# Storing the first softmax maxima by key head, with a shorter lead of maxima before the first scores

## The reference, cut to what matters

```python
q = (x @ Wq + bq).reshape(4, 512, 32, 8)
k = (x @ Wk + bk).reshape(4, 512, 8, 8)      # v likewise; 4 query heads share one key head
attn = softmax(q @ k.T / sqrt(8))            # over 512 keys, per batch and head
out = (attn @ v).reshape(4, 512, 256) @ Wo + bo
```

## Time and profile before

| | |
|---|---|
| median of three executions | 3713.92 us (3711.85 to 3724.83) |
| the profiled execution | 3757.11 us, of which the span from the first to the last instruction is 3755.4 us |
| first maximum of the stage to the last exponential | 1244.3 to about 1731 us of the span |
| first attend of batch 0 | 1274.5 us |
| TensorE, VectorE, ScalarE, GpSimd busy over the whole span | 88%, 70%, 52%, 26% |
| granted TensorE clock, mean of the span | 0.933 of full speed |

### The profile page before, as it was taken

How to read it: one execution, slowest core, us unless ns; L and a number is a source line. 1 busy time by engine, 2 the same in 40 slices (tenths; PEclk the granted TensorE clock), 3 DMA queues, 4 the chain that set the end, 5 groups by cost and what they waited for, 6 DMA issues and landing times. The chain is left out here.

```text
span 3755.4 us, 65204 instructions
## 1 busy us (share of the span) xinstructions
PE 3320.6 (88%) x22154; PEld 2203.1 (59%) x22154; DVE 2622.5 (70%) x8703; ACT 1937.4 (52%) x5275; POOL 990.8 (26%) x960
## 2 busy tenths in 40 slices
PE   6999999986997899997899999988798759999975
PEld 4666676664554344444566676665454437888753
DVE  5888888775444777782788888876444567777765
ACT  4667677654222266675576777655222115555531
POOL 3212112233444001012221212143444333222113
PEclk8999999997999689998999999998999769999986
DMA  4140400012755222302060500011656400000010
GB/s 127 58 160 23 148 1 1 23 44 86 190 90 112 69 53 57 71 3 91 1 216 1 169 1 1 4 44 50 203 90 121 100 1 15 1 15 4 1 33 23
DMA packets 202239, 234.78 MB, mean 63 GB/s; under 512 B 20662, under 2 KB 188536, under 8 KB 201080
## 3 DMA queue, kind: packets, MB, share of 16 engines
q1 hardware_dynamic: 170968, 190.48, 16.7%
q0 software_dynamic: 30944, 40.14, 6.3%
HBM read 98.13 MB, written 133.73 MB: 62 GB/s over the span
## 5 line engine op out<-in xcount | busy, mean ns | idle before, releaser
L1773 ACT ACTIVATE p_prob<-bank,p_small 128x256 f32<-128x256 f32 (+3 forms) x1280 | 647.2, 515 | 151.9 <-DVE p_small L1945 146.7
L1945 DVE CUSTOM_DVE_ANT_0 bank<-bank,p_mask 128x256 f32<-128x256 f32 (+3 forms) x1280 | 579.5, 490 | 145.6 <-PE bank L1516 96.0
L2292 POOL TENSOR_TENSOR p_tm<-p_rope_a,p_rope_b 128x512 f32<-128x512 f32 x192 | 246.3, 1283 | 1273.7 <-DVE p_rope_b L1925 1271.0
L1778 ACT ACTIVATE p_prT<-bank 128x512 f32<-128x512 f32 x752 | 427.4, 602 | 249.5 <-PE bank L1525 203.7
L1516 PE MATMUL bank<-p_k,p_q 64*128 64x256 f32 (+3 forms) x3840 | 530.1, 348 | 20.1 <-ACT p_prob L1773 18.3
L1525 PE MATMUL bank<-g_ident,p_prob 128*128 128x128 f32 x3008 | 448.0, 288 | 66.7 <-DVE p_prob L1954 26.2
L1525 PEld LDWEIGHTS bank<-g_ident,p_prob 128*128 128x128 f32 x3008 | 337.7, 144 | 164.4 <-issue 57.9
L1534 PE MATMUL bank<-p_prT,p_v 128*64 128x512 f32 (+1 forms) x1504 | 431.7, 619 | 1.7 <-issue 1.3
L1954 DVE TENSOR_SCALAR p_prob<-p_prob,p_small 128x256 f32<-128x256 f32 (+3 forms) x1280 | 413.1, 386 | 11.3
L1516 PEld LDWEIGHTS bank<-p_k,p_q 64*128 64x128 f32 (+1 forms) x3840 | 340.0, 189 | 124.8 <-issue 70.7
L1991 DVE TENSOR_REDUCE p_nmax<-bank 128x1 f32<-128x512 f32 x512 | 320.5, 683 | 71.9 <-PE bank L1575 69.9
(11 more groups left out here) (288 smaller groups left out, 6220.7 us busy)
## 6 DMA issues: line engine op xcount, KB each, us to landing
sorted<-p_blank SPq DMA_DIRECT2D x32, 2304.0 KB, 19.3
p_w<-in_L_ffn_w SPq DMA_DIRECT2D x96, 256.0 KB, 4.5
p_h_in<-sorted SPq DMA_DIRECT2D x158, 144.0 KB
p_k_st<-k_saved SPq DMA_DIRECT2D x16, 288.0 KB
p_q_st<-q_saved SPq DMA_DIRECT2D x16, 288.0 KB
g_stage<-in_L_ffn_wq SPq DMA_DIRECT2D x8, 512.0 KB
g_stage<-in_L_ffn_wo SPq DMA_DIRECT2D x16, 256.0 KB
q_saved<-p_qp SPq DMA_DIRECT2D x16, 256.0 KB, 3.2
```

The source lines that it names most:

```text
L1773: act.activation(s.prob.ap[:, 0:s.o.w], s.use.ap[:, 0:s.o.w], ACT.Exp, bias=sm[:, 0, j:j + 1], scale=-1.0, accum_out=sm[:, 1, j:j + 1]).th ...
L1778: act.activation(s.prT.ap, s.use.ap, ACT.Copy).then_inc(s.use.free[0].sem)
L1945: dve.tensor_tensor_reduce(x, x, A.mask[:, A.mask.shape[1] - o.w:], -1.0, FAR, ALU.add, ALU.min, o.sm.ap[:, 0, h.j:h.j + 1]).then_inc(made)
```

## The change

Three things are changed, all in the order of steps of this stage. The first two `qt` of batch 0 store their maxima one key head at a time (`halves`), with smaller slices, so there are 18 stores in place of 16, and an attend waits for the store of its own key head. `LEAD` falls from 48 to 32, and the four additional maxima of batch 0 follow every 16 attends (one key head) in place of every 32; batch 0 thus takes 32 + 8 x 20 = 192 maxima where it took 48 + 4 x 36 = 192, and batches 1 to 3 keep their order. A store and a `finish` are now held back while a `small_product` or `small_values` is half issued (`held`), since all use the one bank of `wring`.

```diff
@@ prelude (small_product; small_values likewise)
                 use = ring.take()
+                held[0] = True
                 for k in range(KC + 1):
...
                     if k < KC:
                         yield
+                held[0] = False
@@ maxima, store_maxima
         def maxima(b, qt):
+            halves = b == 0 and qt < 2
...
-            return lambda: store_maxima(b, qt, s.use)
+                if halves:
+                    store.append(lambda g=g, last=s.use: store_maxima(b, qt, last, cols(g % 2, 1)))
+            if not halves:
+                store.append(lambda: store_maxima(b, qt, s.use, slice(0, 2)))
...
+            n = groups.stop - groups.start
+            k, p = qt % 2, groups.start if n == 1 else qt % 2
+            s.rows, s.nm_p = 2 * KV * n, A.nm_p[p]
...
+            for g in range(groups.start, groups.stop):
+                nm_done[b, 2 * qt + g] = nm_p_read[p]
+        store, held = [], [False]
         def peaks_of_all():
-            store = None
+            since = 0
             for b in range(B):
                 for qt in range(4):
-                    steps = maxima(b, qt)
-                    if store:
-                        for _ in range(4):
-                            next(steps)
-                            yield
-                        store()
-                    store = yield from steps
-            store()
+                    for _ in maxima(b, qt):
+                        yield
+                        since += 1
+                        if store and not held[0] and (since % 16 >= 4 or len(store) > 1):
+                            store.pop(0)()
+            store.pop(0)()
             yield
@@ tick, attend
-                if item[0] < 0:
+                if item[0] < 0 and not (held[0] and item[1].__name__ == "spread"):
...
-                        s.b, s.kv, s.kt, s.r, s.ready = b, kv, kt, r, [nm_done[b, qt], ones_there]
+                        s.b, s.kv, s.kt, s.r, s.ready = b, kv, kt, r, [nm_done[b, kv], ones_there]
@@ the loop
-        LEAD = 48
+        LEAD = 32
...
-                if b == 0:
-                    for _ in range(KV):
-                        next(peaks, None)
+                    if b == 0 and n % 16 == 15:
+                        for _ in range(KV):
+                            next(peaks, None)
```

More of the change, by code:

```diff
@@ L1073, in prelude @@
                 s.t, s.use, s.uh, s.ul, s.va = t, use, uh.ap, ul.ap, va
-                yield
+                if t < T - 1:
+                    yield
+            held[0] = False
+            yield
             uh.users.append(use.full)
@@ L1085, in maxima, with store_maxima @@
                         yield
-            return lambda: store_maxima(b, qt, s.use)
-        def store_maxima(b, qt, last):
-            s = self.step("store_maxima", A)
-            k = qt % 2
-            s.b, s.qt, s.last, s.use = b, qt, last, wring.take()
-            s.after, s.two_after = nm_p_read[k], two_read[k]
-            s.rounded, s.hi, s.lo = (self.vector_made.up() for _ in range(3))
-            nmax_read[k], two_read[k] = s.lo, s.use.full
-            s.count = nm_stored[k]
-            nm_done[b, qt] = nm_p_read[k] = s.count.up(16 * KV)
+                if halves:
+                    store.append(lambda g=g, last=s.use: store_maxima(b, qt, last, cols(g % 2, 1)))
+            if not halves:
+                store.append(lambda: store_maxima(b, qt, s.use, slice(0, 2)))
+        def store_maxima(b, qt, last, groups):
+            s = self.step("store_maxima", A)
+            n = groups.stop - groups.start
+            k, p = qt % 2, groups.start if n == 1 else qt % 2
+            s.b, s.qt, s.last, s.use, s.groups = b, qt, last, wring.take(), groups
+            s.rows, s.nm_p = 2 * KV * n, A.nm_p[p]
+            s.after, s.two_after = nm_p_read[p], two_read[k]
+            s.rounded, s.hi, s.lo = (self.vector_made.up() for _ in range(3))
+            if groups.stop == 2:
+                nmax_read[k], two_read[k] = s.lo, s.use.full
+            s.count = nm_stored[p]
+            nm_p_read[p] = s.count.up(16 * KV)
+            for g in range(groups.start, groups.stop):
+                nm_done[b, 2 * qt + g] = nm_p_read[p]
+        store, held = [], [False]
         def peaks_of_all():
-            store = None
+            since = 0
             for b in range(B):
                 for qt in range(4):
-                    steps = maxima(b, qt)
-                    if store:
-                        for _ in range(4):
-                            next(steps)
-                            yield
-                        store()
-                    store = yield from steps
-            store()
+                    for _ in maxima(b, qt):
+                        yield
+                        since += 1
+                        if store and not held[0] and (since % 16 >= 4 or len(store) > 1):
+                            store.pop(0)()
+            store.pop(0)()
             yield
@@ L1141, in value, with spread @@
                         va.users.append(s.use.full)
-                    later.append([2, lambda: finish(kv, s.o, s.use.free)])
+                    def spread():
+                        finish(kv, s.o, s.use.free)
+                    later.append([2, spread])
             def finish(kv, o, copied):
@@ L1580, in tensor_program @@
             for t in range(T):
-                ins = pe.transpose(s.use.ap[0:16, t * P:(t + 1) * P], A.nm_two[:, s.qt % 2, t].rearrange("p r m g -> p (r m g)"), ident[:, :])
+                ins = pe.transpose(s.use.ap[0:s.rows, t * P:(t + 1) * P], A.nm_two[:, s.qt % 2, t, :, :, s.groups].rearrange("p r m g -> p (r m) g"), ident[:, :])
             ins.then_inc(s.use.full[0].sem)
@@ L1796, in scalar_program @@
             w.wait_ge(s.use.full, s.after)
-            act.activation(A.nm_p[s.qt % 2][:, :], s.use.ap[0:16, :], ACT.Copy).then_inc(s.use.free[0].sem)
+            act.activation(s.nm_p[0:s.rows, :], s.use.ap[0:s.rows, :], ACT.Copy).then_inc(s.use.free[0].sem)
         elif s.kind == "attend":
@@ L1994, in vector_program @@
         elif s.kind == "store_maxima":
-            x, two = A.nmax[:, s.qt % 2], A.nm_two[:, s.qt % 2]
+            x, two, hi = A.nmax[:, s.qt % 2, :, :, s.groups], A.nm_two[:, s.qt % 2, :, :, :, s.groups], A.nm_hi[:, :, :, s.groups]
             w.wait_ge(s.last.free, s.two_after)
-            dve.tensor_copy(A.nm_hi[:, :, :, :], x).then_inc(made)
+            dve.tensor_copy(hi, x).then_inc(made)
             w.wait_ge(s.rounded)
-            dve.tensor_copy(two[:, :, :, 0, :], A.nm_hi[:, :, :, :].bitcast(F32)).then_inc(made)
-            dve.tensor_tensor(two[:, :, :, 1, :], x, A.nm_hi[:, :, :, :].bitcast(F32), ALU.subtract).then_inc(made)
+            dve.tensor_copy(two[:, :, :, 0, :], hi.bitcast(F32)).then_inc(made)
+            dve.tensor_tensor(two[:, :, :, 1, :], x, hi.bitcast(F32), ALU.subtract).then_inc(made)
         elif s.kind == "finish":
@@ L2318, in pool_program @@
         elif s.kind == "store_maxima":
-            qs, np_ = A.q_st[s.b % 2], A.nm_p[s.qt % 2]
+            qs, n = A.q_st[s.b % 2], s.rows // KV
             w.wait_ge(s.use.free)
@@ L2322, in pool_program @@
                 row = r * RT + ROWS
-                pool.dma_start(qs[row:row + 2, 2 * s.qt:2 * s.qt + 2, :].bitcast(F32), np_[4 * r:4 * r + 4, :].bitcast(F32)).then_inc(s.count.sem, 16)
+                pool.dma_start(qs[row:row + 2, 2 * s.qt + s.groups.start:2 * s.qt + s.groups.stop, :].bitcast(F32),
+                               s.nm_p[n * r:n * r + n, :].bitcast(F32)).then_inc(s.count.sem, 16)
         elif s.kind == "small_out":
```

## The result

The changed kernel takes 3739.18 us in the median of 19 runs (3730.02 to 3753.97), the kernel before 3723.06 us in 19 runs beside them (3711.43 to 3732.84). The ratio is 1.0048 with a 95% interval of 1.0035 to 1.006: 0.5% slower. By the ratio that is about 18 us, by the two medians 16. The profiled execution of the changed kernel took 3730.78 us (span 3729.0 us), 26 us less than the profiled one of before. Two single executions thus point the wrong way; they have to be compared inside the stage, from a mark of their own.

The account below looks back on a forecast made before the run. VectorE was taken to set the lead's time and TensorE's in-order queue the attends', except when waiting for banks. Terms -9.6 + 9.6 + 3.0 + 6 = +9.0 us on 3713.9 us gave 3723 us, range 3702 to 3741 us.

Parts of the forecast that it names:

- the likeliest case: Whole kernel: the forecast of 3723 us, 9 us slower, given a chance of 0.50.
- The lead: Before the first attend: 16 maxima fewer at 0.60 us of VectorE each, 9.6 us less.
- Groups and stores: In batch 0: four new groups of four maxima at 2.4 us, +9.6 us; two more stores at 1.5 us, +3.0 us.
- the bound of free banks: Groups in batch 0: lower bound if TensorE never waited for banks, some 0.5 us a group, 2 us in all.
- rival of hidden maxima: In batch 0: spread maxima fit VectorE's idle time unseen by TensorE; -6.6 us, 3707 us, chance 0.25.
- The clock: TensorE in batch 0: new groups bring more time at the lower clock; 0 to 16 us, taken as 6 us.
- The clock-down case: In batch 0: TensorE's clock stays low for nearly all of it; 26 us slower, 3740 us, chance 0.15.
- the border of "slower": Whole kernel: about 0.5% (18.6 us), what a measurement can tell from no change; slower given 0.16.
- The clock-up case: In batch 0: TensorE's clock rises early and stays up; -14 us, or -24 us with hidden groups, 3690 us, chance 0.04.
- Late maxima: First scores and later key heads wait for their maxima; up to 4 us above the forecast, 3727 us, chance 0.06.
- two prices for doubled falls: Four new groups in batch 0, 10 us of low clock each: 16 us at 0.41, 20 us at 0.5.

Follow-up runs that it names:

- Experiment 1: The changed kernel's four stores by key head and guards, with the lead of 48 and groups of four of the kernel before: 3726.1 us, ratio 1.0016 to the kernel before.
- experiment 2: The changed kernel with a lead of 64, no groups of four and stores as before: 3713.94 us, ratio 0.9971 to the kernel before.
- experiments 3 and 6: The 6: like experiment 3, but each maximum picked so that a pair's attends and maxima lie in four different strips: 3773.24 us, ratio 1.005 to the kernel before.
- experiment 3: The changed kernel with batch 0's 32 additional maxima one at a time behind every fourth attend: 3756.96 us, ratio 1.0103 to the kernel before.
- experiment 7: The changed kernel with a lead of 48, stores as before and no additional maxima: 3754.27 us, ratio 0.9986 to the kernel before.

## Why the prediction was right, and where its size was off

The range held, and so did the likeliest case: a little slower, with the groups taking back what the lead gives. The forecast was +9 us; +18 was measured (+16 in the medians). The forecast stood on a median of three runs, 3713.92 us; over 19 runs the kernel before takes 3723.06, so about 9 of the 16 us between 3723 forecast and 3739.18 measured are the starting point and not the change. Step by step:

**The lead.** -9.6 us forecast; 29.5 against 19.9 us from the first reduction, so -9.6. In the second executions it was the same. The first scores did not wait.

**Groups and stores.** +9.6 and +3.0 us forecast, 12.6 in all. In the table D - 0.41 L goes from 109.8 (mean of two executions) to 121.6: +11.8 us. Experiment 1 puts a store inside batch 0 at 1.9 us, which leaves 8.0 us for four groups, 2.0 each. Taking the groups away in experiment 2 gave back 6.9 us for four (109.8 to 102.9), 1.7 each. So a group costs 1.7 to 2.0 us and not 2.4, a store a little more than 1.5, and the two errors nearly cancel. The copies to `nm_p` are 18, six of them within batch 0's attends. The prediction named the bound of free banks as 0.5 us for a group, so the choice of the upper value was right. That the maxima are no cheaper one by one (experiments 3 and 6) shows that the rival of hidden maxima falls.

**The clock.** This is the term that was mis-sized: "I take a little over a third of the upper bound, 6 us". Over all timed executions, and not the profiled ones alone, the mean granted clock of the span is known: 0.9350 in the 29 runs of before beside the first experiments, 0.9313 in the 19 of the changed kernel. 0.0037 / 0.5 x 3730 us is 28 us more at the lower clock. The lead has to be taken out of this. It is at the lower clock throughout (0.50 in both tables) but VectorE sets its time, so its low time costs nothing, and the changed kernel has 9.6 us less of it. Some 37 us more of low time thus lie where it costs, at 0.41 us each 15 us. With it the sum is -9.6 + 11.8 + 15 = +17 us against the 18 measured; the interval of the ratio stands for 13 to 22 us. The same sum, of a kernel's lead, its order in the four batches and its mean clock, comes within 6 us of each of the nine timed sets of the experiments and inside its interval, or at its edge: for instance -5 us against -11 for experiment 2, +37 against +38 for experiment 3, +35 against +34 for a lead of 80.

So the clock term was nearly the whole upper bound of 16 us. The reason for taking a third had been that new falls may lie within low stretches that exist already. Mostly they did not: in the profiled executions L went from 41 and 61 us to 73 and 68. These alone would give (70.2 - 51.0) x 0.41 = 8 us, so about half of the 15 us is seen in batch 0, and where in the span the rest of the low time lies is not shown. The runs compared were not all made side by side, and the 0.41 comes from batch 0's loop. As a check on it, within the 29 runs of before a us more of low time goes with 0.42 us more of time and within the 19 of the changed kernel with 0.40, but within the runs of before on the two other chips with 0.30 and 0.28. The 15 us is an estimate, with 10 as its low end.

**The rivals.** The clock-down case was close. It was to decide from about 38 us of additional low time on, and some 37 came; its 26 us were too much, and L did not reach the 126 us of the batch, except nearly in experiment 3, where 111 us of it went with the ratio 1.0103. By the ratio, the measured loss stayed less than 1 us below the 18.6 us named as the border of "slower", which is luck. The clock-up case was not seen. Late maxima were not seen in the changed kernel, but they exist: experiment 7 has them.

**The Trainium skill on TensorE's clock.** Without groups the falls behind the first stretch nearly go (17.7 us of low time in both executions with a lead of 64, against 51 and 70 with four and eight groups), and with work in the groups' waits there are 29 us less of low time in one execution. The rule that cycling through banks with small idle times makes the clock go back and forth (the Trainium skill, TensorE: Matmul & The Clock Gate, "A second HAM failure mode: psum-queue depth-cycling") is borne out by both. Of the prediction's two prices for doubled falls, the 16 us at 0.41 was close to the 15 found; the estimate of 20 us, at the half that the same page of the Trainium skill gives, was too much.

**What stays open.** Why the same group is followed by a short fall in one execution and by a long one in another is not explained by anything in these traces. Nor is it settled how much of lead 80's loss the waits for loads make.

## What to carry to other kernels

Moving work from a head start into a loop is free only if the loop's pacing queue does not wait for it. Here each of the 16 moved maxima held up TensorE's in-order queue for 0.43 to 0.50 us of the 0.60 us of VectorE that it had cost in the lead, and the low clock behind the waits made it a loss. Taking all additional maxima out of the loop, which lengthens the head start by 9.6 us, was the faster kernel (0.9971 and 0.9979 in two timings). When a kernel's clock falls by chance, compare single profiles by a stage's time less a fixed share of its low-clock time, leave out low time in stretches that another engine paces, and judge the clock itself by many runs.

## What the runs showed of the hardware that was not expected

The granted clock after one group of four maxima differed between executions of one program: 0.94 and 0.56 over the same 32 attends, 12 us apart. Blocks of products of zeros, issued where TensorE would have stood still, kept the clock up in part (43.5 us of low time against 72.7 and 67.6) although they compute nothing, and in the mean of 12 runs brought it back to about that of the kernel before (0.9331 beside 0.9322). And an order in which pairs of small matmuls meet in the same 32-row strips of the array, which started 0.59 us apart at the lower clock where four in different strips start together, went with 111 us of low clock in a batch of 166 us, and with a mean clock of 0.9253 over 6 runs beside 0.9350; in D - 0.41 L the collision itself cost nothing that can be seen (120.3 us against 121.3).
